# Attention in a decoder layer: stationary operands of 100 to 121 bf16 columns widened to 128

## The reference, cut to what matters

```python
q = (query @ Wq + bq).reshape(B, Nq, H, D)...      # Nq 100, H 16, D 16
k = (key_value @ Wk + bk).reshape(B, Nkv, H, D)... # Nkv 361
attn = jnp.einsum('bhqd,bhkd->bhqk', q, k) * scale
attn = jnp.clip(attn, -CLAMP, CLAMP)
attn = jax.nn.softmax(attn, axis=-1)
x = jnp.einsum('bhqk,bhkd->bqhd', attn, v).reshape(B, Nq, Cq)
return x @ Wo + bo
```

## Time and profile before

| | us |
|---|---|
| three runs | 1611.31, 1612.80, 1620.85 |
| median of the three | 1612.8 |
| the profiled execution's own time | 1611.83 |
| its span, first to last instruction | 1609.9 |

### The profile page before, as it was taken

How to read it: one execution, slowest core, us unless ns; L and a number is a source line. 1 busy time by engine, 2 the same in 40 slices (tenths; PEclk the granted TensorE clock), 3 DMA queues, 4 the chain that set the end, 5 groups by cost and what they waited for, 6 DMA issues and landing times. The chain is left out here.

```text
span 1609.9 us, 31655 instructions
## 1 busy us (share of the span) xinstructions
PE 1367.0 (85%) x9914; PEld 947.0 (59%) x9915; DVE 1020.0 (63%) x2361; ACT 553.0 (34%) x1356; POOL 786.4 (49%) x1072
## 2 busy tenths in 40 slices
PE   4788778877746998999998899999986699999996
PEld 2455555545534666666666666666664366666664
DVE  2687987798741777888787888888875122222221
ACT  1333323323311345444354444444442112122221
POOL 3234643463343557766666666777664122222222
PEclk9999999999975899999899999999995799999999
DMA  4992000000005655656555564655551122222222
GB/s 148 304 321 60 1 1 1 0 0 1 1 0 92 93 85 106 117 113 107 109 103 115 109 113 96 111 117 118 112 110 38 39 45 44 46 46 46 44 45 23
DMA packets 180329, 128.01 MB, mean 80 GB/s; under 512 B 69010, under 2 KB 173090, under 8 KB 180194
## 3 DMA queue, kind: packets, MB, share of 16 engines
q1 hardware_dynamic: 167890, 112.23, 33.0%
q0 software_dynamic: 12304, 14.10, 5.8%
HBM read 36.10 MB, written 44.83 MB: 50 GB/s over the span
## 5 line engine op out<-in xcount | busy, mean ns | idle before, releaser
L1327 DVE TENSOR_REDUCE neg_raw<-bank_s 100x2 f32<-100x722 f32 x256 | 231.0, 902 | 97.4 <-PE bank_s L1536 86.5
L1220 ACT ACTIVATE prob<-bank_st 120x400 f32<-120x400 f32 (+1 forms) x384 | 166.3, 512 | 190.1 <-PE bank_st L1553 190.1
L1877 POOL DMA_INDIRECT out<-result,target x57 | 88.2, 1547 | 266.6 <-DVE result L1851 263.7
L1338 DVE TENSOR_SCALAR bank_st<-bank_st 120x400 f32<-120x400 f32 (+1 forms) x384 | 195.3, 570 | 0.2 <-issue 0.2
L748 PE MATMUL bank_l<-q_heads,k 128*100 128x192 f32 (+4 forms) x512 | 119.3, 372 | 65.4 <-DVE attn L562 52.2
L1075 POOL TENSOR_TENSOR neg_diag<-xident_b,neg_max 100x400 bf16<-100x400 bf16 x128 | 109.4, 855 | 124.7 <-DVE neg_max L1332 116.4
L1862 DVE TENSOR_TENSOR hidden<-silu,ebank_v 128x512 f32<-128x512 f32 x57 | 39.2, 688 | 196.7 <-PE ebank_v L1786 196.7
L1536 PE MATMUL bank_s<-k_st,q_st 96*100 96x361 bf16 x512 | 130.6, 337 | 35.0 <-DVE neg_raw L1327 21.4
L748 PEld LDWEIGHTS bank_l<-q_heads,k 128*100 128x100 f32 x512 | 79.0, 172 | 113.8 <-DVE attn L562 43.2
L396 ACT ACTIVATE q_heads<-q 32x192 f32<-32x192 f32 (+3 forms) x168 | 62.1, 370 | 224.4 <-DVE q L521 221.4
L1544 PEld LDWEIGHTS bank_st<-q_st,k_st 96*120 96x120 bf16 (+1 forms) x1536 | 109.9, 137 | 22.2 <-ACT prob L1220 10.9
(11 more groups left out here) (203 smaller groups left out, 2724.7 us busy)
## 6 DMA issues: line engine op xcount, KB each, us to landing
k_st<-k_part SPq DMA_DIRECT2D x384, 90.2 KB
slot_rows<-empty SPq DMA_DIRECT2D x9, 2967.0 KB, 26.3
q_st<-q_part SPq DMA_DIRECT2D x384, 25.0 KB
kv<-in_ctx_t SPq DMA_DIRECT2D x32, 270.8 KB
expert_w<-in_w SPq DMA_DIRECT2D x16, 512.0 KB, 4.1
rows<-slot_rows SPq DMA_DIRECT2D x57, 129.0 KB
residual<-in_w SPq DMA_DIRECT2D x16, 256.0 KB, 4.5
residual<-in_x SPq DMA_DIRECT2D x8, 400.0 KB
```

The costliest lines, as they stand in the source:

```text
L1220: act.activation(prob[0:KEYS[c], t % 2, c], bank_st[c][0:KEYS[c], 0:4 * T], ACT.Exp).then_inc(exp_done, 1)
L1327: dve.tensor_reduce(neg_raw[:, h:h + 2], bank_s[0:T, :, 0:S], AX.X, ALU.max, negate=True).then_inc(max_done, 1)
L1338: dve.tensor_scalar(tile, tile, CLAMP, -CLAMP, ALU.min, ALU.max).then_inc(clipped, 1)
```

## The change

Each bf16 stationary operand of `scores`, `scores_t` and `shift` becomes 128 columns wide. To read 128 columns, a head's queries run on into the next head's, and a chunk's keys into the next chunk or head; `q_st` and `k_st` lose their head axis and get 28 and 8 columns of zeros at the end, so that the last head also has 128 to read. The products write 128 PSUM rows instead of 100, 121 or 120. DVE and ACT read the same rows as before, and nothing reads the surplus ones. The moving operands, the count and the order of PE's instructions, DVE's and ACT's work, and the shapes of SP's copies are unchanged. POOL gets two fills more (96x56 and 96x16 elements), and `consts` counts 12 instead of 10.

In the built program each of the 2432 bf16 loads reads its columns as four groups of 32, where before it read one row of 100, 120 or 121. The f32 loads are built as before.

```diff
+WIDE = 128
+Q_OVER = WIDE - 100
+K_OVER = KEY0[2] + WIDE - S
...
-        q_st = sb("q_st", [96, 2, NH, T], BF16)
-        k_st = sb("k_st", [96, 2, NH, S], BF16)
+        q_st = sb("q_st", [96, 2, NH * T + Q_OVER], BF16)
+        k_st = sb("k_st", [96, 2, NH * S + K_OVER], BF16)
...
-        CONSTS = 10
+        CONSTS = 12
...
-                        sp.dma_start(dst[row:row + 16, p, 8 * c:8 * c + 8], part[:, parts, c]).then_inc(done, 16)
+                        heads8 = dst[row:row + 16, p, 8 * c * n:8 * (c + 1) * n].rearrange("p (h n) -> p h n", h=8)
+                        sp.dma_start(heads8, part[:, parts, c]).then_inc(done, 16)
...
+            pool.memset(q_st[:, :, NH * T:], 0.0).then_inc(consts, 1)
+            pool.memset(k_st[:, :, NH * S:], 0.0).then_inc(consts, 1)
             pool.memset(val[:], 0.0).then_inc(consts, 1)
...
-                    mm = pe.matmul(bank_s[0:T, i, 0:S], q_st[:, p, h], k_st[:, p, h], start=True, stop=True)
+                    mm = pe.matmul(bank_s[0:WIDE, i, 0:S], q_st[:, p, h * T:h * T + WIDE],
+                                   k_st[:, p, h * S:(h + 1) * S], start=True, stop=True)
...
-                    mm = pe.matmul(bank_st[c][0:KEYS[c], j * T:(j + 1) * T],
-                                   k_st[:, p, h, KEY0[c]:KEY0[c] + KEYS[c]], q_st[:, p, h], start=(j == 0),
+                    at = h * S + KEY0[c]
+                    mm = pe.matmul(bank_st[c][0:WIDE, j * T:(j + 1) * T], k_st[:, p, at:at + WIDE],
+                                   q_st[:, p, h * T:(h + 1) * T], start=(j == 0),
                                    stop=False, skip_group_check=True)
...
-                pe.matmul(bank_st[c][0:KEYS[c], 0:4 * T], ones_b[:, 0:KEYS[c]],
+                pe.matmul(bank_st[c][0:WIDE, 0:4 * T], ones_b[:],
```

More of the change, by code:

```diff
@@ L959, in spread @@
                 def spread(dst, part, slots, parts, c, done):
+                    n = part.shape[3]
                     for slot in slots:
                         row = 16 * slot
-                        sp.dma_start(dst[row:row + 16, p, 8 * c:8 * c + 8], part[:, parts, c]).then_inc(done, 16)
+                        heads8 = dst[row:row + 16, p, 8 * c * n:8 * (c + 1) * n].rearrange("p (h n) -> p h n", h=8)
+                        sp.dma_start(heads8, part[:, parts, c]).then_inc(done, 16)
                 until(st_summed, 12 * (b - 1))
@@ L1032, in _ @@
             pool.memset(earlier[:], 0.0).then_inc(consts, 1)
-            pool.wait_ge(consts, 7)
+            pool.wait_ge(consts, 9)
             pool.memset(val[:, :, :, 0:17 * NH].rearrange("p a c (h d) -> p (a c) h d", d=17)[:, :, :, 16:17],
```

## The result

| | us |
|---|---|
| before, four runs | 1611.31, 1612.05, 1612.80, 1620.85; median 1612.42 |
| after, four runs | 1640.40, 1641.25, 1648.17, 1648.73; median 1644.71 |
| ratio, 95% interval | 1.0185 [1.0157, 1.0213] |
| profiled execution of after: its own time, its span | 1641.25, 1639.3 |

A forecast was written before the change was run, and what follows sets the result against it. PE and DVE were taken to alternate as the bound in the attention stage. 32 elements x 0.21 us = 6.7 us off 1611.8 gave 1605.1; with the median 1.0 us higher, 1606 us, range 1595 to 1620.

The forecast's parts named there:

- The fast load: 128-column bf16 loads vanish behind the stream: 0.12 us a `scores_t` group, up to 0.03 us each exposed load.
- plain load: Rival: 128 columns are loaded one a cycle, costing 2.3 us, 1615 us; chance 0.10.
- no overlap: Rival: the fast load does not overlap the running product, 1637 us taken; chance 0.06.
- What of it is on the path: On PE's stretch and the 714.21 hand-over, one group and three loads count: 0.21 us an element, 6.7 us.
- The groups at t = 1, 2 and 3 lie off the path: In the attention stage, these groups' savings only lengthen PE's waits of 0.34, 0.32 and 0.96 us; no gain counted.
- DVE's own lengths: DVE's steps in the attention stage keep their length; a change in them would show the prediction wrong; no size given.
- The clock: Rival: PE's waits grow 0.4 us an element, one to three more falls, 1609 to 1618 us; chance 0.10.
- needs six or more: Clock rival's condition for a slowdown past 1%: six or more extra falls, each 3 to 5 us.

The follow-up runs named there:

- e1: Changed kernel with DVE's slots addition moved behind `negated` at t = 0, where POOL is idle; 1607.01 us, 0.9959.
- e13: Changed kernel with the slots addition folded into DVE's one-input sum, POOL writing `first_slot` into a ninth column of `chosen`; 1605.20 us, 0.9923.
- e11: Kernel before, loads narrow, with one tiny addition more on POOL ahead of `neg_diag` at t = 0; 1658.67 us, 1.0268.
- e8: Changed kernel with the slots addition moved behind `negated` at t = 0 and `row`'s normalisation behind `negated` at t = 3; 1621.06 us, 1.0019.
- e4: Changed kernel with 127 columns in place of 128 everywhere; 1626.47 us, 1.0083.
- e6: Changed kernel with 128 columns in `scores` alone; 1612.97 us, 0.9986.
- e5: Changed kernel with 128 columns in `scores_t` alone; 1630.26 us, 1.0096.
- e7: Changed kernel with PE's wait before the second `scores` pair at t = 0 filled with ten products that nothing reads; 1621.33 us, 1.0039.
- e12: Changed kernel with one small single-column reduction more on DVE ahead of the slots addition; 1643.79 us, 1.0186.
- e3: Changed kernel with DVE's sum of `slot_f` made twice, delaying the slots addition; 1653.12 us, 1.0264.
- e10: Kernel before, operands narrow, with DVE's sum of `slot_f` made twice; 1620.51 us, 1.0036.

## Why the prediction was wrong, step by step

- **The fast load: right.** Group 0.70 us, pair of `scores` 0.48, and no faster load with 127 columns. The rivals "plain load" and "no overlap" fell: 45 ns from start to start is less than the load of 128 columns one a cycle, and the products of one group follow each other on the same 96 rows. The Trainium skill (TensorE: Matmul & The Clock Gate, Weight-path perf modes) asks for 128 weights that are not FP32; the runs with 128 and 127 agree, at 45 and 58 ns.
- **What of it is on the path: the total agrees, the way to it isn't shown.** Forecast 6.7 us; 5 and 8.6 us in two pairs of kernels, 12 in the third, each uncertain by 4 us or more. The forecast wanted each element 0.21 us shorter; the two pairs of traces show 0.02 us shorter and 0.02 us longer. So part of the agreement is the clock, or luck.
- **"The groups at t = 1, 2 and 3 lie off the path ... and the waits ... grow by what they save": the step that failed.** It let a saving vanish into a wait. The saving at t = 3 also moves `shift`, ACT's exponents and `kf` behind it, and with `kf` the counting product (L1617), which DVE takes with a wait of 0.37 us before and 0.22 after. So `slots` begins 0.14 us earlier against POOL's `neg_diag`, is held for 1.9 us, and the time rises by 32.3 us instead of falling by 6.7. A product that is early by itself costs nothing; who takes it then runs at another time, beside another neighbour.
- **DVE's own lengths.** Every length in the sum was taken as fixed. The prediction did name a change of DVE's steps as what would make it wrong, but had no price for it. The row for it stood in the trace of before: one `slots` of 2149 ns among 16, right before the wait of 1.63 us in the earlier trace rows. I read that wait and did not ask what DVE was doing in it. Moving or folding the addition takes the whole loss away (e1, e13), and 0.14 us on POOL brings more than all of it to the narrow kernel (e11).
- **The clock: the mechanism right, the number wrong.** "Waits longer by 0.4 us, one to three more falls, each 3 to 5 us." The waits that counted were not the ones that grew by 0.1 us but 11 new ones of some 1.7 us. By the clock record 5 stretches at half clock began in the attention stage (71.7 us), and 12 begin in it now (126.3 us); with the wait filled they are 4 (64.9 us). In each count one of 41 us begins at the stage's end and lies in the experts' stage. The falls cost 23.4 us. Past 1% "needs six or more": seven came, with the additions' own 14.3 us.

## What to carry to other kernels

Where two engines can hold each other up, a saving upstream is also a shift in time: before calling it hidden, list the instructions that would start earlier or later, look at who runs beside them, and look for outliers in the length of one repeated small instruction (minimum, median and maximum of a group), since one of them in 16 tells that an edge is near. A two-input operation on DVE in a place where timing can slide is worth turning into a one-input reduction, even if it is only 400 numbers; here that also turned a 1.9% loss into a 0.8% gain. One input alone is no safeguard: `row` has one tensor as input and takes 1.4 us beside POOL and 0.40 away from it (e8). And a short wait of PE in a busy stretch can be dearer through the clock than through its own length: fill it to find out.

## What the runs showed of the hardware that I had not expected

**DVE waits for POOL, and longer than one of its instructions.** Length of the addition by what was left of POOL's running instruction when it began, from the traces:

| kernel | left | addition, us |
|---|---|---|
| before | 0.106 to 0.132 of `neg_diag` | 0.16 |
| before, once | 0.469 | 2.15 |
| e4 | 0.044 to 0.067 of `neg_diag` | 0.16 |
| e6 | 0.117 to 0.143 | 0.16 |
| after | 0.197, 0.212 | 0.215, 0.229 |
| after | 0.255 to 0.266 | 1.93 to 1.95 |
| after, once | 0.510 | 2.19 |
| e5 | 0.182 to 0.197 | 0.20 to 0.22 |
| e5 | 0.230, 0.231 | 0.249 |
| e5 | 0.232 to 0.238 | 1.91 to 1.92 |
| e11 | 0.252 to 0.265 | 1.93 to 1.95 |
| e4 to e7, e11, e12, once each | 0.41 to 0.61 | 2.09 to 2.28 |
| e12, once | 0.131 | 0.153 |
| e12 | 0.166 to 0.194 | 1.84 to 1.87 |
| e3 | 0.036 to 0.050 of `neg_diag`, `kr` just beginning | 1.71 to 1.73 |
| e3, twice | 0.81 to 0.82 of `kr` | 0.83 |
| e10 | 0.73 of `kr` | 0.75 |

Long ones end with the instruction `k_part`, after which POOL pauses 0.14 us, or with `kr`. The distance alone doesn't decide: with 0.044 us left the addition was short in e4, and with as much left it was long in e3. It goes the other way round too: in e4 `kr` begins 0.08 us after the short addition's start and up to 0.036 us after `neg_diag` has ended, where in before it begins 0.04 us ahead of that end. There it is POOL that waits. The one-input sums beside the same POOL work stay at 0.19 us (e13). The Trainium skill (GPSIMD Engine Reference, Specifications) says that GpSimd's SBUF interfaces are shared with VectorE and contended for by VectorE instructions in a 2-port mode or with two SBUF inputs; the runs agree, 1.93 us with two inputs and 0.19 with one. The Trainium skill (SBUF — State Buffer, SBUF: two separate sides) also says that whichever instruction starts first holds the shared pair for its whole length. The rows agree that the addition is not served in the middle of one, but by that rule alone it would wait for the 0.26 us left of `neg_diag`, not for `kr` and `k_part` as well, 1.93 us. Why it is let in at the end of `kr` in e10 and of `neg_diag` up to 0.231 us left, but not otherwise, stays open; no run here settles it. That the two meet at SBUF, and not elsewhere, is the Trainium skill's account; the runs show who waits for whom, and how long.

**The price of a wait at PE.** Waits of PE of some 1.7 us were followed by half clock behind 9 of the 12 long additions, and by none where ten products filled them (e7). The half clock cost more (23.4 us) than the delay by itself (14.3 us).

**Noise.** The mixer, which no edit touches, has 71.7 us at half clock before and 85.3 after, and up to 102 in other kernels, with the attention stage's first products starting between 498.1 and 505.4 us. That is some 3.5 us either way in a single run, and the reason why the smaller differences above are given as intervals.
